# A fused state-space layer: joined decay scans, chunk ends computed once, and an out product by tokens

## What is computed

```python
x = rmsnorm(layernorm(h)) * norm_w
z, xBC, dt_raw = split(x @ in_proj_w)          # 2048, 3072, 32 columns
xBC = silu(causal_conv4(xBC) + conv_b)
xs, B, C = split(xBC)                          # 32 heads x 64, 8 groups x 64, 8 groups x 64
dt = softplus(dt_raw + dt_bias);  dA = exp(-dt * exp(A_log))
for t in range(512):
    state = dA[t] * state + (dt[t] * xs[t]) * B[t]
    y[t]  = state @ C[t]
g = groupwise_rmsnorm((y + D * xs) * silu(z)) * gate_norm_w
h = h + layernorm(h) + g @ out_proj_w          # the layer has its own residual inside
out = h + ternary_ffn(layernorm(h))            # 128 -> 512 -> gelu -> layernorm -> 128
```

## Time and profile before

| | us |
|---|---|
| median of 3 runs | 1143.55 (1142.07 to 1146.34) |
| the profiled execution, its own time | 1145.73 |
| its span, first to last instruction | 1143.9 |
| TensorE busy | 1033.2 (90%) |
| VectorE busy | 1059.9 (93%) |
| ScalarE busy | 970.0 (85%) |
| GpSimd busy | 868.6 (76%) |

### The profile page before, as it was taken

The page is one execution under the profiler, slowest core; times in us unless marked ns, Lnnn a source line. Parts: engine busy times, 40 slices in busy tenths (PEclk is TensorE's granted clock), DMA queues, the critical chain, the costliest instruction groups (busy, mean ns, idle before and its releaser), DMA issues.

```text
span 1143.9 us, 26227 instructions
## 1 busy us (share of the span) xinstructions
PE 1033.2 (90%) x8912; PEld 732.0 (64%) x8912; DVE 1059.9 (93%) x2004; ACT 970.0 (85%) x2836; POOL 868.6 (76%) x596
## 2 busy tenths in 40 slices
PE   1724789999999999999999999999999999996797
PEld 1603566676666666676666666766666666664576
DVE  7597999999999999999999999999999999989474
ACT  2767898999999999999999999999999999984464
POOL 7300356888888888888888888888888888885765
PEclk9955899999999999999999999999999999997899
DMA  6320000000000000000000000000000000021001
GB/s 170 117 86 0 10 1 2 1 1 2 1 30 2 2 2 29 2 2 2 29 2 2 2 29 2 2 2 29 2 1 1 21 1 2 1 78 46 1 29 46
DMA packets 28084, 22.58 MB, mean 20 GB/s; under 512 B 11696, under 2 KB 22576, under 8 KB 27824
## 3 DMA queue, kind: packets, MB, share of 16 engines
q1 hardware_dynamic: 25136, 20.90, 5.9%
q10 hardware_dynamic: 2816, 0.02, 0.1%
HBM read 12.78 MB, written 8.13 MB: 18 GB/s over the span
## 4 chain that ended last, share of the span: by engine, by line
PE 77%; DVE 14%; issue 3%; POOL 2%; ACT 2%; DMA 0%; POOLq 0%; DVEq 0%; ACTq 0%
PE bank L1713 10%; PE bank L1695 10%; PE bank L1625 8%; PE bank L1727 8%; PE bank L1641 8%; PE bank L1626 6%; PE bank L1627 6%; PE bank L1681 5%; PE bank L1662 5%; DVE conv L1191 4%; PE bank L1766 3%; PE bank L1738 2%; DVE lm L1181 2%; PE bank L1555 1%; PE bank L1746 1%
## 5 line engine op out<-in xcount | busy, mean ns | idle before, releaser
L1191 DVE SCALAR_TENSOR_TENSOR conv<-bank,cw,conv 128x509 f32<-128x509 f32 (+2 forms) x576 | 421.7, 743 | 16.6 <-ACT conv L762 8.6
L636 POOL TENSOR_TENSOR lm<-lm,cbs 128x1024 f32<-128x1024 f32 x128 | 304.3, 2377 | 75.7 <-ACT xw L866 75.7
L1181 DVE TENSOR_TENSOR_SCAN lm<-bank,ident 128x512 f32<-128x512 f32 x256 | 298.7, 1210 | 0.7 <-PE bank L1641 0.6
L911 ACT ACTIVATE xdt<-bank,dt_all 128x64 f32<-128x64 f32 x1024 | 222.3, 329 | 37.2 <-PE bank L1662 37.2
L866 ACT ACTIVATE xw<-xdt,lm 128x64 f32<-128x64 f32 x768 | 199.3, 365 | 0.0
L644 POOL TENSOR_TENSOR ssum<-ssum,sq 128x512 f32<-128x512 f32 x96 | 123.1, 1283 | 93.0 <-ACT sq L926 92.8
L1625 PE MATMUL bank<-xn_hi,w_hi 128*128 128x512 f32 x320 | 166.1, 519 | 13.8 <-DVE conv L1191 13.1
L615 POOL TENSOR_TENSOR gated<-gated,gate 128x512 f32<-128x512 f32 x128 | 164.9, 1288 | 15.9 <-DVE gated L1238 14.5
L626 POOL TENSOR_TENSOR gated<-gated,rbs 128x512 f32<-128x512 f32 x120 | 153.8, 1282 | 0.0
L877 ACT ACTIVATE conv<-bank,cb_bias,cw 128x512 f32<-128x512 f32 x189 | 142.6, 781 | 11.5 <-PE bank L1627 7.3
L1713 PEld LDWEIGHTS bank<-lm,xdt 128*64 128x64 f32 x2048 | 110.3, 137 | 63.7 <-issue 63.7
(11 more groups left out here) (217 smaller groups left out, 1766.5 us busy)
## 6 DMA issues: line engine op xcount, KB each, us to landing
lm<-in_L_attn_in_proj_w SPq DMA_DIRECT2D x1, 2048.0 KB, 11.7
xn_scratch<-chan SPq DMA_DIRECT2D x4, 512.0 KB, 4.6
r_stage<-residual_scratch SPq DMA_DIRECT2D x8, 256.0 KB, 2.9
xn_stage<-xn_scratch SPq DMA_DIRECT2D x7, 256.0 KB, 3.2
x_scratch<-r_stage SPq DMA_DIRECT2D x7, 256.0 KB, 2.0
gate<-in_L_attn_hidden_states SPq DMA_DIRECT2D x2, 512.0 KB, 4.6
cdec<-in_L_attn_hidden_states SPq DMA_DIRECT2D x2, 512.0 KB, 7.1
w_out<-in_L_attn_out_proj_w SPq DMA_DIRECT2D x8, 128.0 KB, 3.3
```

What stands on the lines that cost most here:

```text
L636: gp.tensor_tensor(lm[:, mr, :, :], lm[:, mr, :, :], cbs[:, :, :], ALU.mult).then_inc(m_done, 1)
L911: act.activation(xdt[:, r, at:at + HP], misc_of("xt", n)[:, at:at + HP], ACT.Copy, scale=dt_h).then_inc(xdt_done, 1)
L1181: V.tensor_tensor_scan(lm[:, m % R, a, :], bc_bank[(3 * m + a) % 2][:, :], ident4[:, :], 0.0, ALU.mult, ALU.add).then_inc(scanned, 1)
L1191: V.scalar_tensor_tensor(out=conv[:, ci % 4, shift:S], in0=tile_bank(b, n, t)[:, 0:S - shift], scalar=cw[:, q, t, KW - 1 - shift:KW - shif ...
```

## The change

Five edits, and what follows from them:

1. **One scan for both heads.** The two decay banks become one PSUM tensor `decays` of 1024 columns, `ident4` holds the identity eight times, and one scan over 1024 columns replaces two. Rows k = 0 and k = 1 now always lie in the first and second half, and k = 2 in the second, behind the scan.
2. **Chunk ends once.** `pend` holds them for all slots and batches. Behind slot 4 of the first batch, 16 small products into `out_bank` and one copy on VectorE fill it; the copy in every slot goes.
3. **First state on ScalarE.** `first_state` copies it from PSUM; VectorE keeps the two steps.
4. **Norm factors expanded on GpSimd**, right behind its power in `root`, in place of ScalarE's `expand_root`.
5. **Out product by tokens.** `gated` is the stationary side, in four pieces of 128 tokens, and the slot's part of `w_out` the moving side of 128 columns. The result has tokens in partitions; ScalarE's copy and TensorE's transposes go, VectorE adds the residual straight from `out_bank`, right behind the scan of slot 15, and the next batch's first out product waits for that.

`dtb`, `alog` and `aexp` move into `qdiag`'s memory. The core of the diff:

```diff
-        ident4 = sb("ident4", [P, S])
+        ident4 = sb("ident4", [P, 2 * S])
-        pend = sb("pend", [P, 4, CH])
+        pend = sb("pend", [P, SLOTS, NCH])
-        bank = [pb(f"bank{i}", [P, S]) for i in range(8)]
+        low = [pb(f"bank{i}", [P, S]) for i in range(2)]
+        decays = pb("decays", [P, 2 * S])
+        bank = low + [decays[:, S * i:S * i + S] for i in range(2)] + [pb(f"bank{i}", [P, S]) for i in range(4, 8)]
...
                     gp.tensor_tensor(rtok[:, :], vtok[:, :], neghalf[:, 0:2 * CH], ALU.pow).then_inc(rstd_done, 1)
+                    after(gp, rstd_done, UNITS, bb, v)
+                    after(gp, rbc_ready, UNITS, bb, v - 1)
+                    gp.tensor_copy(rexp[:, :, :], rtok[:, :].unsqueeze(2).broadcast_to([P, 2 * CH, HP])).then_inc(rexp_done, 1)
...
+                def first_state():
+
+                    if back(b, n, LAG_STATE) is None:
+                        return
+                    bb, m = back(b, n, LAG_STATE)
+                    after(act, s_ready, SLOTS, bb, m)
+                    after(act, y_ready, SLOTS, bb, m - 2)
+                    act.activation(hpk[:, m % 2, 0, :], misc_of("s", n)[:, 0:NS], ACT.Copy).then_inc(hfirst, 1)
...
-                    for a in range(2):
-                        after(dve, bc_ready, 3 * SLOTS, bb, 3 * m + a)
-                        V.tensor_tensor_scan(lm[:, m % R, a, :], bc_bank[(3 * m + a) % 2][:, :], ident4[:, :], 0.0,
-                                             ALU.mult, ALU.add).then_inc(scanned, 1)
+                    after(dve, bc_ready, 3 * SLOTS, bb, 3 * m + 1)
+                    V.tensor_tensor_scan(lm[:, m % R, :, :].rearrange("p a s -> p (a s)"), decays[:, :], ident4[:, :], 0.0,
+                                         ALU.mult, ALU.add).then_inc(scanned, 1)
...
+                def output_rows():
...
+                    after(dve, out_step, SLOTS, bb, SLOTS - 1)
+                    dve.wait_ge(res_loaded, bb * 16 + 16)
+                    xs = r_stage[:, :, :]
+                    V.tensor_tensor(xs, out_bank[:, :].rearrange("p (c d) -> p c d", d=DM), xs, ALU.add).then_inc(x1_done, 1)
...
                 slot(0, n)
+                if n == R:
+                    dve.wait_ge(pend_ready, 1)
+                    V.tensor_copy(pend[:, :, :].rearrange("p m c -> p (m c)"), out_bank[:, :]).then_inc(pend_done, 1)
...
-                i = 3 * m + k
-
-                pm, pk = divmod(i - 2, 3)
-                if pk < 2:
-                    after(pe, scanned, 2 * SLOTS, bb, 2 * pm + pk)
+                if k == 1:
+                    after(pe, cdec_done, SLOTS, bb, m - 1)
                 else:
-                    after(pe, cdec_done, SLOTS, bb, pm)
+                    after(pe, scanned, SLOTS, bb, m - 1 if k == 0 else m)
...
                     if m == 0:
-                        after(pe, out_copied, 1, bb, -1)
-                    last = MM(out_bank[:, :], w_out[:, m, :], gated[:, (m // R) % 2, m % R, :], start=(m == 0), stop=(m == SLOTS - 1))
+                        after(pe, x1_done, 1, bb, -1)
+                        if bb == 0:
+                            pe.wait_ge(pend_done, 1)
+                    for c in range(CH):
+                        tok = slice(P * c, P * c + P)
+                        last = MM(out_bank[:, tok], gated[:, (m // R) % 2, m % R, tok], w_out[:, m, :],
+                                  start=(m == 0 and c == 0), stop=(m == SLOTS - 1 and c == CH - 1))
...
+                if n == R:
+                    ends = pr_parts[:, :].rearrange("k (c i) -> k c i", i=P)[:, :, P - 1:P].rearrange("k c i -> k (c i)")
+                    for m in range(SLOTS):
+                        last = MM(out_bank[:, NCH * m:NCH * m + NCH], sel[:, m, HP:HP + P], ends, start=True, stop=True)
+                    last.then_inc(pend_ready, 1)
```

120 lines of the change are left out of this document (37 added, 83 removed).

## The result

| | before | changed kernel |
|---|---|---|
| median, us | 1144.94 (1142.07 to 1146.34, 4 runs) | 1160.66 (1157.60 to 1161.21, 4 runs) |
| profiled execution, us | 1145.73 | 1160.25 |
| its span, us | 1143.9 | 1158.4 |

The ratio is 1.0135, with a 95% interval of 1.0106 to 1.0164: slower by 1.4%, some 15.7 us. The prediction was 1146.2 us, with 1156 as its upper end.

The account below looks back on a forecast made before the run. TensorE's own work was taken to set the steady time, VectorE trailing. Terms 2.6 - 4.2 + 1.4 + 0 + 0.8 + 2.0 = +2.6 us gave 1148.3 profiled, 1146.2 us as median; own range 1141 to 1152, whole range 1135 to 1156.

Parts of the forecast that it names:

- The joined scan's waits: Steady units: VectorE starts late in the second slot, recovers before the fourth slot's decay row with 0.16 us spare; cost 0.
- TensorE waits for the joined scan: Rival at the fourth slot's decay row: beyond 0.16 us extra VectorE lag every unit is slower; 1156 us, chance 0.14.
- The wait in slot 15: First out product of a batch waits for VectorE's residual addition: +0.2 us in each of 7 batches, +1.4 us.
- The out product by tokens: TensorE's four 128-column products replace one of 512 columns: +0.02 us in each of 128 slots, +2.6 us.
- The output transposes: Four TensorE transposes leave slot 15 of each of eight batches: -5.0 us, decay row behind them +0.8, together -4.2 us.
- that rival: Token-wise out product on TensorE: weight loads partly open, +18 us instead of +2.6, 1161 us; chance 0.09.
- the one that follows the rule of the Trainium skill: Token-wise out product: every weight load stands in front of its product, +0.8 us times 128, 1250 us; chance 0.01.
- VectorE's savings: Copies removed and scans joined save VectorE 0.21 us a slot, 27 us in all, worth nothing in the steady part.
- D: Follow-up theory that VectorE sets the pace: three edits relieving it would give plain units of 28.0 us or less.
- the third rival: VectorE is the bound after all, so its savings make the program faster: 1137 us, down to 1112; chance 0.12.
- The ramp: Program start: 16 small chunk-end products and their copy delay VectorE by 2.9 us, ten slots return 2.1; +0.8 us.
- The tail: Program end: joined scan on the chain +1.1 us, GpSimd expansion before the root +0.9 us; together +2.0 us.

Follow-up runs that it names:

- the split run: Changed kernel with its scan split in two, decay rows in fixed halves, TensorE's wait for both scans kept: 1150.10 us, ratio 1.0041 to the kernel before.

## Why the prediction was wrong, step by step

**The joined scan's waits, "0, but tight": the step that failed.** The rival "TensorE waits for the joined scan" had the place, the decay row in slot D, and the threshold, 0.16 us of extra lag. The start in slot B was also right: I had VectorE lose 0.77 us there, and it lost 0.80 (6.65 against 5.85 us into the unit). What failed is the recovery after it, the saving of 0.21 us a slot. From B's scan to D's I had counted 16.02 us less two such savings, 15.60; it took 15.77 (385.12 to 400.89). So a slot saves 0.12, not 0.21.

VectorE's own rows show where the rest went. Start to start, the joined scan gave 0.04 (2.21 in place of 2.25) and the two copies 0.20 (0.13 and 0.07), more than I had counted. But 0.10 came back behind the first tap. Before, from the first tap of slot B on:

```profile
381.99 0.75 DVE L1191 SCALAR_TENSOR_TENSOR conv<-bank,cw,conv 128x511 f32<-128x511 f32 x1
382.66 0.21 DVE L1210 COPY hpk<-bank 128x64 f32<-128x64 f32 x1
382.79 0.74 DVE L1191 SCALAR_TENSOR_TENSOR conv<-bank,cw,conv 128x510 f32<-128x510 f32 x1
```

The same two taps in the changed kernel, each from a narrow window:

```profile
387.33 0.73 DVE L1184 SCALAR_TENSOR_TENSOR conv<-bank,cw,conv 128x511 f32<-128x511 f32 x1
388.09 0.75 DVE L1184 SCALAR_TENSOR_TENSOR conv<-bank,cw,conv 128x510 f32<-128x510 f32 x1
```

The second tap adds to what the first has written, and in the kernel it waits for the first one's semaphore. With the copy between them, each step starts 0.08 us before the one ahead of it has ended. Without it the second tap starts 0.03 us after the first has ended, so 0.76 us after its start, where another step came after 0.67. The steady parts of all profiles agree. In the ten with the first state on ScalarE, three times a unit a tap stands directly behind the tap of the same tile that it waits for, and each time it comes 0.75 to 0.79 us after it; directly behind a tap of another tile it comes after 0.64 to 0.70. In the seven in which VectorE keeps the first state, no two such taps are neighbours, and none comes later than 0.66. So the copy had filled a wait of one tap for another: taking it away gave 0.13 us and took 0.10 back. In the runs with two scans and the first state on ScalarE a second wait of that size stands in front of the first state step, and from B's scan to D's they take 16.02 to 16.18 us, no less than before. That this wait is the cause is read from these rows; no run keeps the first state on ScalarE and puts other work between the two taps.

That closes the count. I had the last scan end 24.53 us into the unit (484.81, the unit's variance record starting at 460.28); it ended at 24.71, the row started 0.06 us later, a step that I had at nothing, and so at 24.77 in place of the 24.66 of the split run. The slack of 0.16 us was gone. The sign that I had named for being wrong, a wait of over 0.1 us in slot D, is there with 0.11. I should have given a reserve of 0.16 us on a path of 18 us, repeated in every unit, far more than a chance of 0.14. My reading of the waits also left out a line: before, TensorE's loads for the products with the state waited 8.9 us for VectorE's state steps, 21 times in 800 us; so VectorE was closer behind TensorE than I said. In the changed kernel these are 21.2 us, 50 times.

**The wait in slot 15, +1.4, measured 3 us.** Most of it is the same lag a second time. The addition stands behind the late scan, and the out product waits for it. The chain of the changed kernel at the end of a batch (start us, us, what):

```profile
546.11 2.20 DVE lm L1174
548.31 0.59 DVE r_stage L1238
548.91 0.14 issue
549.04 1.13 PE bank L1678 x8
```

The row ahead of it starts at 548.37, so the out product comes 0.67 us behind the row where a plain unit has 0.22 (403.24 to 403.46). TensorE pays 0.45 us per batch in place of 0.2; with two scans in fixed halves it is 0.06. There this unit is 28.85 instead of 29.34, and so 6 x 0.49 us of the steady loss are here, with 0.13 for the seventh. The other 21 units lose 0.12 each. Together that is 5.6 us, and 5.5 lie between the two steady stretches (813.0 and 807.5).

**The out product by tokens, +2.6.** Right in kind, a third too small: 0.12 us a unit, 3.8 us over 32. In the chain it is 0.89 us (at 403.63) where I had 0.88. **The output transposes, -4.2**: 0.44 a batch by the slot-15 unit, -3.5. The two cancel, as the run with them alone shows. Weight loads stayed covered: 8 full-height loads and 8 passes in 0.89 us, so that rival falls, and with it the one that follows the rule of the Trainium skill.

**VectorE's savings worth nothing**: right while the scan is split, and D and the third rival fall with it. **ScalarE 0** missed one thing: the first state delays the scaling of x. That costs 0.21 us a batch where output transposes wait for it; in the changed kernel nothing does. **GpSimd's expansion**: 0.61 us where I took 0.9 (ScalarE had 0.62, not the 0.49 that an expectation above gives), and nobody waits for it in steady units.

**The ramp, +0.8, measured +3.3.** The copy of the chunk ends came at 122.82 where I had 121.7, after VectorE had idled 3.86 us. TensorE was at its lower clock there: from 117 to 123 us the granted clock was 0.50, before it was 0.94, and the 16 C-B products ahead took 2.08 us in place of 1.16. I had taken their time from before. Nothing of the loss came back. With split scans the ramp is 201.7, so 2.3 of the 3.3 go with the joined scan, some clock included; between 110 and 200 us VectorE waits 1.7 us for second rows in it. The rest is within what the clock moves.

**The tail, +2.0, measured +5.7.** The joined scan cost its 1.1: in the changed kernel's chain it is 2.30 us, against 1.24.

```profile
1046.46 2.30 DVE lm L1174
1048.80 0.61 PE decays L1620
```

The expansion cost 0.6 by the "last" column where the clock stays up (63.5 against 62.9), and 3.3 more are the clock, below; I had left one us for it. The remaining 0.7 us lie ahead of the last variance product, where the tail takes 74.6 us against 72.8. With two scans in alternating banks it takes 72.8 again, so they too go with the joined scan; how they arise stays open.

Of the spans, then: between the changed kernel and its version with two scans in fixed halves lie 11.0 us (1158.4 and 1147.4). Of these 3.2 are in the last part, where the clock fell in the one execution alone, which leaves 7.8: 2.3 in the ramp and 5.5 in the steady units. The 1.8 us ahead of the last variance product that version still pays (74.7), as TensorE waits for both scans in it too. With them the joined scan is between 9 and 10 of the 14.5 us, and most of the rest is the expansion and the clock in the tail.

## What to carry to other kernels

Joining two operations saves a fixed cost, here 0.05 us of VectorE's time, and charges the wait for the later of the two inputs; find what issues that input, and if it stands last in its queue, price the whole wait. When the producer paces the program and the consumer trails by a tenth of a microsecond, look at how much the consumer can recover before the two meet again, and treat a reserve smaller than the error of that sum as spent. Work taken out may have stood between two steps of which the second waits for the first; look at what becomes neighbours. Moving the input earlier in a full queue is no free repair: it may meet another wait, or a neighbour that it overlaps less well.
